# A depthwise 5x5 convolution joined with its pointwise mix: from 128x128 band matrices to sixteen 32x32 tiles of TensorE

## The reference

```python
qkv = einsum('bchw,oc->bohw', ln_c(x), w_qkv)                 # 192 channels = 24 groups of 8
dw  = conv(qkv, w_dw, 5x5, padding 2, one filter per channel)
pw  = einsum('bgihw,goi->bgohw', dw in 24 groups of 8, w_pw)  # 8 in, 8 out, inside a group
att = relu_linear_attention(concat([qkv, pw]))                # 16 heads: 8 of qkv, 8 of pw
x   = x + batchnorm(einsum('bchw,oc->bohw', att, w_proj))
t   = tokens(x)
t   = t + sum over 8 experts of w[e] * (gelu(ln(t) @ W1[e] + b1[e]) @ W2[e] + b2[e])   # top 2 of 8
```

## Time and profile before

| what | before |
|---|---|
| median of 3 runs | 125.72 us (125.64 to 126.02) |
| the profiled execution, its own time | 125.97 us |
| its span in the profile | 124.3 us |
| PE busy | 119.4 us (96%) |
| PEld busy | 94.9 us (76%) |
| DVE busy | 88.6 us (71%) |
| ACT busy | 84.9 us (68%) |
| POOL busy | 29.4 us (24%) |

### The profile page before, as it was taken

The page is one execution under the profiler, slowest core; times in us unless marked ns, Lnnn a source line. Parts: engine busy times, 40 slices in busy tenths (PEclk is TensorE's granted clock), DMA queues, the critical chain, the costliest instruction groups (busy, mean ns, idle before and its releaser), DMA issues.

```text
span 124.3 us, 2671 instructions
## 1 busy us (share of the span) xinstructions
PE 119.4 (96%) x918; PEld 94.9 (76%) x918; DVE 88.6 (71%) x279; ACT 84.9 (68%) x197; POOL 29.4 (24%) x34
## 2 busy tenths in 40 slices
PE   6998999999999999999999999999999999999991
PEld 5397899999999889896786786666766767666660
DVE  0689999999987887998896039994607236077972
ACT  4479999999972948259797499194690947919300
POOL 7308999900000000303370005000000000000370
PEclk9999999999999999999999999999999999999999
DMA  3779400000000000000000038961069891001001
GB/s 101 217 176 228 136 3 0 3 5 0 0 0 0 5 0 0 0 5 0 0 0 3 7 69 233 235 148 45 11 167 221 228 235 41 5 3 42 0 0 42
DMA packets 5590, 8.11 MB, mean 65 GB/s; under 512 B 1442, under 2 KB 4042, under 8 KB 5578
## 3 DMA queue, kind: packets, MB, share of 16 engines
q1 hardware_dynamic: 5344, 7.80, 25.2%
q10 hardware_dynamic: 234, 0.15, 0.4%
HBM read 7.36 MB, written 0.59 MB: 64 GB/s over the span
## 4 chain that ended last, share of the span: by engine, by line
PE 80%; DVE 7%; ACT 4%; DMA 3%; issue 2%; POOL 1%; POOLq 1%; SPq 0%; DVEq 0%
PE PS L975 53%; PE PS L1204 17%; PE PS L1091 3%; DMA X<-in_x_dram 3%; DVE BAND L870 2%; DVE STATS L610 2%; PE PS L1097 2%; ACT MS L433 1%; PE PS L1128 1%; POOL XP L416 1%; PE PS L1114 1%; PE PS L1159 1%; PE PS L1051 1%; DVE XP L906 1%; DVE WY L896 1%
## 5 line engine op out<-in xcount | busy, mean ns | idle before, releaser
L538 ACT ACTIVATE MS<-PS,B 128x512 f32<-128x512 f32 x48 | 29.1, 689 | 7.2 <-PE PS L975 6.9
L975 PE MATMUL PS<-QP,BAND 128*128 128x120 f32 (+2 forms) x240 | 27.0, 275 | 0.2 <-DVE QP L666 0.2
L975 PEld LDWEIGHTS PS<-QP,BAND 128*128 128x128 f32 x240 | 26.9, 192 | 0.4 <-issue 0.4
L975 PE MATMUL PS<-XS,W1H 128*128 128x512 f32 x64 | 26.5, 414 | 0.0
L975 PE MATMUL PS<-XS,W1L 128*128 128x512 f32 x64 | 25.3, 395 | 0.0
L1204 PE MATMUL PS<-MS,W 128*64 128x256 f32 x192 | 22.3, 383 | 0.0
L846 DVE SCALAR_TENSOR_TENSOR WY<-PS,B,BAND 128x256 f32<-128x256 f32 x24 | 10.5, 480 | 15.2 <-PE PS L1204 14.5
L1204 PEld LDWEIGHTS PS<-MS,W 128*64 128x64 f32 x192 | 13.2, 137 | 8.5 <-ACT MS L538 1.5
L456 ACT ACTIVATE BAND<-RS,PW 128x80 f32<-128x80 f32 x64 | 17.3, 447 | 0.0
L975 PEld LDWEIGHTS PS<-XS,W1H 128*128 128x128 f32 x64 | 12.0, 188 | 4.8 <-issue 0.9
L975 PEld LDWEIGHTS PS<-XS,W1L 128*128 128x128 f32 x64 | 12.1, 189 | 1.8
(11 more groups left out here) (128 smaller groups left out, 168.2 us busy)
## 6 DMA issues: line engine op xcount, KB each, us to landing
BAND<-spread_dram SPq DMA_DIRECT2D x14, 256.0 KB, 4.8
W<-in_w_dram SPq DMA_DIRECT2D x3, 512.0 KB, 6.4
X<-in_x_dram SPq DMA_DIRECT2D x2, 256.0 KB, 3.7
BAND<-spread_dram SPq DMA_DIRECT2D x4, 128.0 KB, 3.2
out_dram<-XP SPq DMA_DIRECT2D x4, 128.0 KB, 1.7
W<-spread_dram SPq DMA_DIRECT2D x2, 256.0 KB, 5.7
VEC<-in_vectors_dram SPq DMA_DIRECT2D x1, 132.0 KB, 3.0
SELF<-in_select_dram ACTq DMA_DIRECT2D x1, 100.8 KB
```

Of the source, the lines that this page charges most:

```text
L538: act.activation(hidden(n), PS[:, h_bank(n), :], ACT.Gelu, bias=B1[:, k:k + 1]).then_inc(gelu_done, 1)
L975: return pe.matmul(PS[0:parts, bank, cols[0]:cols[1]], lhsT, rhs, start=start, stop=stop)
```

## The change

The convolution is computed with weights of 32x32: four columns of x times eight channels on both sides. The sixteen columns form four blocks, and an output block takes its own block and its two neighbours (off = 0, 1, -1). So there are 15 steps (five dy, three off) for each of q, k and v, and each step is 16 calls, one for each tile of the array: row tile r and column tile c. A row tile holds one group of four heads' values, a column tile gives one of two groups g and one of two halves of the images. A call moves 2 x (8 or 6) x (14 to 16) columns. The row tiles write four PSUM banks, the column tiles four strips of partitions.

The values reach that layout by transposes on PE: scaled qkv now goes to MSQ (channel order by head and column), `turn_heads` turns it into PSUM, `fill_qp` (DVE and ACT) copies it to QP; the results go through `take_conv` (DVE and ACT) to CV, `turn_back` turns them, and `second_v`, `second_k`, `second_q` read them from PSUM into VM, KR and MS. The order is v, k, q. The transposes of the input for the residual move from ahead of the convolution into it. The band matrices are smaller (BANDS, 30 x 96 columns) and all made by POOL. `rs` makes 32 products of 30 columns in float32 from unrounded w_dw. Six warm-up products stand before `qkv`. POOL copies the first half of q into MS. The splitting of W1 on DVE stands between `second_v` and the taking of the second convolution; `centred_residual` moves between `read_kv(0)` and `read_kv(1)`. The part from `kv(2)` on is unchanged.

```diff
+SPAN = 11
+BLOCK = 4
+SHIFTS, FIRST_SHIFT, PADDED = 8, -2, 12
...
-        WARM_UPS, TILE_BANKS = 3, (7, 5)
-        RS_BANKS = (3, 4, 5, 7)
+        WARM_UPS, WARM_UPS_BEFORE_QKV, TILE_BANKS = 3, 6, (7, 5)
+        RS_BANK = 3
+        TURNED_BANKS = (0, 1), (2, 6), (3, 4)
+        CONV_BANKS = (5, 7, 0, 1), (2, 6, 3, 4), (5, 7, 0, 1)
+        BACK_BANKS = (5, 7), (2, 6), (3, 4)
...
 POOL
+            pool.memset(BANDS[:, :, 0:2 * I], 0.0).then_inc(zeros_set, 1)
+            pool.memset(BANDS[:, :, (PADDED - 2) * I:PADDED * I], 0.0).then_inc(zeros_set, 1)
...
+            for r in range(4):
+                rows = slice(32 * r, 32 * r + 32)
+                pool.tensor_copy(PWQ[rows, :, :, :], PW[rows].rearrange("p (g r q) o -> p r q g o", g=2, r=4)[:, r])\
+                    .then_inc(pwq_made, 1)
+            pool.wait_ge(rs_copied, 1)
+            for n in range(3):
+                for g in range(2):
+                    pool.tensor_tensor(*band_factors(2 - n, g), ALU.mult).then_inc(band_p, 1)
...
+            for s in range(PAIRS):
+                pool.tensor_copy(MS[:, 4 * s:4 * s + 4, 0:HH]..., first_half(s, 0)).then_inc(q_first, 1)
 ACT
-            bands(2)
-            bands(5)
-            bands(8)
...
+            fill_qp(0)
+            fill_qp(1)
+            fill_qp(2)
...
+            for s in range(3):
+                first_heads(s)
+            take_conv(0)
+            first_heads(3)
             split_high()
...
+            take_conv(1)
+            for k in range(2):
+                second_k(k)
+            take_conv(2)
...
+            second_q(0)
+            second_q(2)
             relu_qt(0)
             relu_qt(1)
-            second_heads(3)
 DVE
-            link(dve.tensor_copy(WD[:, :], WDF[:, :]))
...
+            def fill_qp(n):
+                dve.wait_ge(heads_turned, 2 * n + 1)
+                dve.tensor_copy(QP[:, 2 - n, 0, :], PS[:, TURNED_BANKS[n][0], :]).then_inc(qp_v, 1)
+            def take_conv(n):
+                for r in (0, 1):
+                    dve.wait_ge(conv_ready, 4 * n + r + 1)
+                    dve.tensor_copy(CV[:, n, r, :], PS[:, CONV_BANKS[n][r], 0:256]).then_inc(cv_v, 1)
...
+            fill_qp(0)
+            fill_qp(1)
+            fill_qp(2)
+            dve.wait_ge(cst_in, 16)
+            take_conv(0)
+            for k in range(2):
+                second_v(k)
+            dve.wait_ge(w_high, 2)
+            split_low(0)
+            split_low(1)
...
+            take_conv(1)
+            normalisation()
+            residual()
+            take_conv(2)
...
+            second_q(1)
+            second_q(3)
             read_kv(0)
-            split_low(1)
+            centred_residual()
             read_kv(1)
 PE
+            rs()
+            warm_up(WARM_UPS_BEFORE_QKV, TILE_BANKS[1])
             pe.wait_ge(wqc_copied, 1)
...
+            TAPS = [(off, dy) for dy in (PAD, 0, 1, 3, 4) for off in (0, 1, -1)]
+            def conv(n, between):
+                q = 2 - n
+                pe.wait_ge(band_p, 2 * n + 2)
+                for m, (off, dy) in enumerate(TAPS):
+                    if m in between:
+                        between[m]()
+                    y0, y1 = max(0, PAD - dy), min(H, H + PAD - dy)
+                    t0, t1 = max(0, -off), min(BLOCK, BLOCK - off)
+                    for r in range(4):
+                        rows = slice(32 * r, 32 * r + 32)
+                        for c in range(4):
+                            g, half = divmod(c, 2)
+                            at = BLOCK * I * (1 - off)
+                            i = pe.matmul(
+                                PS[32 * c:32 * c + 32, CONV_BANKS[n][r], 0:256]
+                                .rearrange("p (s t y) -> p s t y", s=2, t=8)[:, :, 2 * t0:2 * t1, y0:y1],
+                                BANDS[rows, DY * (2 * q + g) + dy, at:at + BLOCK * I],
+                                QP[rows, q, g, :].rearrange("p (s t y) -> p s t y", s=4, t=8)
+                                [:, 2 * half:2 * half + 2, 2 * (t0 + off):2 * (t1 + off), y0 + dy - PAD:y1 + dy - PAD],
+                                start=m == 0, stop=m == len(TAPS) - 1)
+                        if m == len(TAPS) - 1:
+                            i.then_inc(conv_ready, 1)
+            pe.wait_ge(scaled_v, 4)
+            pe.wait_ge(scaled_s, 4)
+            turn_heads(0, (0, 2), False)
+            turn_heads(1, (0, 2), False)
+            pe.wait_ge(scaled_v, 8)
+            pe.wait_ge(scaled_s, 8)
+            turn_heads(0, (1, 3), True)
+            turn_heads(1, (1, 3), True)
+            turn_heads(2, range(PAIRS), True)
+            pe.wait_ge(qp_v, 1)
+            pe.wait_ge(qp_s, 1)
+            conv(0, {})
+            pe.wait_ge(qp_v, 3)
+            pe.wait_ge(qp_s, 3)
+            conv(1, {6: lambda: turn_back(0)})
...
+            pe.wait_ge(v_more, 4)
+            conv(2, {6: turn_k_and_input})      # turn_back(1), then turn_input()
...
-            pe.wait_ge(conv_moved, 9)
+            kv(0)
             pe.wait_ge(xb_ready, 2)
-            kv(0)
-            pe.wait_ge(conv_moved, 10)
+            turn_back(2)
+            pe.wait_ge(cv_v, 6)
+            pe.wait_ge(cv_s, 6)
+            kv(1)
             qt(0)
             qt(1)
-            kv(1)
             num(0)
```

More of the change, by code:

```diff
@@ L49 @@
 C_END = C_IOTA + E
[L50 removed]
 LOW = 64
+SPAN = 11
+BLOCK = 4
+SHIFTS, FIRST_SHIFT, PADDED = 8, -2, 12
+LATE_SIZE = 6400
 def constants():
@@ L160, in build @@
         ONEHOT = late(2, 16, E)
-        WB = late(2, E, N)
         def hidden(n):
@@ L541, in _, with second_q @@
             act.wait_ge(b1_in, 16)
-            def second_heads(s):
-                relu_k(s, 1)
-                if s >= 1:
-                    for b in range(2):
-                        to, of, one = masked_v(s, 1, b)
-                        act.activation(to, of, ACT.Copy, scale=one).then_inc(v_more, 1)
-            second_heads(0)
-            second_heads(1)
-            second_heads(2)
+            def second_q(s):
+                act.wait_ge(back_turned, 4 + s % 2 + 1)
+                act.activation(MS[:, 4 * s:4 * s + 4, HH:HD], second_half(2, s), ACT.Copy).then_inc(q_s, 1)
+            second_q(0)
+            second_q(2)
             relu_qt(0)
             relu_qt(1)
-            second_heads(3)
             copy_attt(0)
@@ new lines, in turn_back @@
+            def turn_back(n):
+                pe.wait_ge(cv_v, 2 * n + 2)
+                pe.wait_ge(cv_s, 2 * n + 2)
+                for k in range(2):
+                    for r in range(4):
+                        i = pe.transpose(PS[:, BACK_BANKS[n][k], :]
+                                         .rearrange("p (x g r o) -> p r g x o", x=8, g=2, r=4)[:, r],
+                                         CV[:, n, r, 128 * k:128 * k + 128], IDT[:, :])
+                    i.then_inc(back_turned, 1)
```

343 lines of the change are left out of this document (142 added, 201 removed).

## The result

The changed kernel takes 147.73 us (median of 4 runs, 146.18 to 150.99) against 125.84 us for the kernel before beside it: a ratio of 1.169 (95% interval 1.165 to 1.173). The ratio leaves out the run of 150.99 us, which had a lower clock (0.954) than the other three. The prediction said 121.7 us and a range from 119.5 to 128. It was wrong in sign and in size.

A forecast was written before the change was run, and what follows sets the result against it. PE's chain was taken as the bound. The convolution ends 6.4 us earlier, 2.3 us is lost behind it, so 4.1 us less: 121.9 from the profiled 125.97, 121.7 us as a median; range 119.5 to 128.

The forecast's parts named there:

- What bounds the kernel now: Whole kernel: PE's chain sets the time; moving the first feed-forward matmul (55.19 us) earlier moves the end as much.
- Ahead of the convolution: Before the first tile: transposes of all three parts on PE start the convolution at 14.3 for 13.15, +1.15 us.
- They are hidden under what follows: Before the convolution: POOL's six band products, about 0.65 us each, done by 12.3, cost nothing on the path.
- C: Rival: PE's clock falls to 1.2 GHz for 4 us of the convolution, costing 2 us: 123.7 us; chance 0.08.
- The convolution, 19.4 us: Convolution from 14.3 to 33.7 us: tiles 15.0, transposes 2.65, changes of tile shape 0.6, wait for DVE 1.2.
- 15.0 in all: Convolution's tiles: sixteen work side by side, a step lasts one call, 5.0 us a part, 15.0 against 27.0.
- A's mild and strong forms: Rival, convolution tiles not fed: mild 18 to 24 us, 123.5 to 129.5 (0.20 with B); strong over 129.5 (0.12).
- B: Rival, fetching PE's convolution instructions: ten packets, 23 us if each is asked for late, time 128.5; shares 0.20.
- 24 transposes, the changes between shapes, the wait for DVE: Inside the convolution: transposes 2.65 us, four changes between small tiles and whole array 0.6, wait at `turn_back(1)` 1.2.
- Behind it, +2.3: From convolution's end to the feed-forward part: new transposes and DVE's centring ahead of `read_kv(1)` cost 2.3 to 2.4 us.

The follow-up runs named there:

- eight_pool_later: Changed kernel with eight tiles of 512 columns in place of sixteen, and POOL's copies and bands begun only after DVE's scaling factors: 136.88 us (1.086 of before).
- eight_tiles: Changed kernel with eight float32 tiles of 512 columns in place of sixteen, so half the calls for the same products: 138.1 us.
- double_columns: Changed kernel with every convolution call moving all four image pairs (up to 512 columns in place of 256), same instructions: 150.21 us.
- eight_bf16: Changed kernel with eight bfloat16 tiles of 512 columns (720 small instructions) and POOL's work begun after DVE's scaling factors: 123.05 us (0.977 of before).
- pool_later: Changed kernel with one added wait: POOL begins its copies and bands only after DVE's scaling factors: 144.73 us (1.151 of before).
- half_columns: Changed kernel with fourteen of each part's fifteen steps moving one image pair in place of two, same instructions: 148.68 us.

## Why the prediction was wrong

*What bounds the kernel now:* right. PE's chain gave the time, and the feed-forward part kept its length: 69.1 and 69.0 us.

*Ahead of the convolution, +1.15, was +4.93.* Two sentences failed. "They are hidden under what follows", of POOL's bands: each took 0.76 us for my 0.65, and the work that should hide them, DVE's, was slowed by them; I had looked at whether the bands come in time, never at what runs beside them. Before, POOL began its bands at 9.73, at the end of DVE's small operations, so no row of before showed the two together; that start was the difference to look at. The other was C: I gave it 0.08 and had it strike in the tiles, while it struck in the transposes ahead of them, for 1.7 us where I named 2. With POOL's overlap taken away the step is right (14.13 and, in `eight_pool_later`, 14.39 for 14.3).

*The convolution, 19.4 us, was 41.76.* The step that failed is "15.0 in all": that a step lasts as long as one call. It priced the array and left the supply to the rivals. More than eight tiles do work side by side: by my price of 0.845 ns a column, `eight_tiles` (30.3 us without its transposes) had 7.9 matmuls going at a time and `double_columns` (40.5) 11.9, an estimate. That all sixteen do, as the 15.0 needs, no run shows. My own row for eight was weaker than I took it: two rounds of 512 columns would be 0.87 us at that price, and the warm-up took 1.9. In bursts a pair took 19 ns (128 in 2.4 us), above my 10.4 and already enough for 27 us. But sustained it was 29 ns. A's mild and strong forms, 18 to 30 us, fell short of it, and eight side by side, as A's strong form had it, was not the cause. B named the true mechanism and half of its signature (17 packets for 7, but never abutting), and I bounded it at 23 us from 10 packets of 1.14 us and "as much again for its start". What was mis-sized: the packets are 11; one takes 3.73 us from one burst to the next where I had 2.3; and each was asked for too late to keep PE busy, which I had as the worse of two cases. Beside the transfer the period holds 1.0 us ahead of it and some 1.5 behind it; what they are made of the runs don't show. The earlier trace rows gave no rate at all, since the kernel before used an instruction in 56 ns (480 in 26.96 us): a bound from a resource that nothing had loaded should have been left open upwards, by the nearest sustained row (65 ns a pair, 94 us), with a far larger chance than the 0.12 beyond 129.5.

The Trainium skill (Runtime: NRT & Kernel Launch, "Instruction fetch mechanics") gives blocks of 256 instructions, which the bursts agree with. It calls the cost of crossing a block mostly hidden; here 11 us of a stage of 42 are standstills, so the measurement decides. Nor did eight blocks lie ready, as the prediction read from it, but some 360 instructions. Its floor of about 25 ns between starts of matmuls (TensorE: Matmul & The Clock Gate, "Wait — 56ns, not 53.3ns?") would have given a time near 141.5, nearer than mine, by another mechanism: within bursts the starts were 19 ns apart, and only the mean over the standstills is 29 ns.

*24 transposes, the changes between shapes, the wait for DVE.* Transposes and changes together took 2.92 us (35.63 to 36.65 and 50.24 to 52.14) for my 3.25. The wait, 1.2 us, didn't come, as A had it: a slower stage takes it away. It came back as 3.28 us once the stage was fast (`eight_bf16`).

*Behind it, +2.3, was +2.12:* right, and by its own rows. DVE in the kernel after:

```profile
63.32 1.21 DVE L694 TENSOR_REDUCE XBM<-XB 128x16 f32<-128x1024 f32 x1
64.56 1.23 DVE L695 SCALAR_TENSOR_TENSOR XB<-XBM,XB 128x1024 f32<-128x1024 f32 x1
65.82 0.59 DVE L723 TENSOR_TENSOR KV<-PS,CST 64x128 f32<-64x128 f32 x2
```

The centring stands ahead of `read_kv(1)`, which ends at 66.6, +6.85 from the end of the convolution, where I had +6.95.

## What to carry to other kernels

Small tiles side by side trade array time for instructions. Before trading, divide the stage's forecast by its count of PE instructions, loads included: a stage that asks for one in less than about 15 ns over more than a few hundred of them gets its length from the count, as it did here (2880, 42 us; 1440, 21 us), and fewer, wider calls or a type with one pass are worth more than more tiles, as long as the other engines can take the results in time. When a resource was never loaded in the trace, its share there is no bound on its rate. And when work is moved onto an engine that "has time", look at what runs beside it, and at what the moved work delays later: POOL's bands first slowed DVE, and moved out of its way they delayed POOL's powers.

## What the runs showed of the hardware

- PE's instructions arrived 256 at a time, one 16 KB packet for each, about every 3.7 us (3.73, 3.73, 3.83 us between bursts; 3.45 to 4.00 in `pool_later` and `half_columns`), 14.6 ns an instruction, at either clock, with float32 and bfloat16, with eight tiles and sixteen. Some 360 were ready at the start of the stage. A block's transfer started 1.0 us after the block before it came into use.
- DVE operations of 16 columns with two inputs in SBUF took 0.71 to 0.80 us in place of 0.17 while POOL multiplied tensors in SBUF, one for each of POOL's operations. How many were caught varied from two to five between executions.
- A pause in which PE had 1.06 us of work in 2.75 was followed by a clock of 0.53 for 3.65 us; with 24 transposes in one row of 2.96 us (`pool_later`), or a pause of 0.28 us (`half_columns`), it wasn't.
- A call of one column by one column cost 62 ns (two matmuls, two loads), at a clock near half, though 64 calls on small tiles had started within 0.69 us (6.32 to 7.01), 11 ns a pair.
- 181 matmuls of 32x32 tiles with up to 256 columns, in float32, took 3.36 us, and 1440 of up to 512 columns 40.5: by estimate 11.9 at a time there, where eight tiles had 7.9.
